# SyncE's wait for the output stores, moved from inside the block of engine programs to behind it

## What is computed

```python
x = x + L0(x, cond)   # base weight plus 8 low-rank experts, mixed by cond
x = x + L1(x, cond)   # x @ (sum over g of cond[b,g] * weight[g] * mask) + bias
x = x + L2(x, cond)   # top-2 of 8 gated-GELU experts per batch, hidden size 512, plus a shared one
x = x + L3(x, cond)   # the top-1 expert: down(silu(up(x)) * gate(x)), hidden size 256
```

## Time and profile before

| what | value |
|---|---|
| median of 3 runs | 86.92 us (86.73 to 87.36) |
| the profiled execution, its time | 87.03 us |
| its span, first to last instruction of the program | 85.2 us |
| time outside the span in that execution | 1.8 us |
| granted TensorE clock | 1.0 of full speed |
| PE busy | 82.0 us, 96% of the span |
| output stores | 8 of 64 KB each |

### The profile page before, as it was taken

The page is one execution under the profiler, slowest core; times in us unless marked ns, Lnnn a source line. Parts: engine busy times, 40 slices in busy tenths (PEclk is TensorE's granted clock), DMA queues, the critical chain, the costliest instruction groups (busy, mean ns, idle before and its releaser), DMA issues.

```text
span 85.2 us, 1938 instructions
## 1 busy us (share of the span) xinstructions
PE 82.0 (96%) x620; PEld 77.6 (91%) x620; DVE 48.5 (57%) x115; ACT 31.7 (37%) x59; POOL 15.8 (19%) x20
## 2 busy tenths in 40 slices
PE   6999999999999999999999999999999999999980
PEld 6879998888889989999999999999999999999960
DVE  1487798845336996446438428438446555463170
ACT  6502795875558401123121221221212302407450
POOL 3020298389666700000000000000000000000000
DMA  1995000699990001884879899988899898607002
GB/s 15 387 388 221 0 0 0 211 415 400 421 382 28 0 0 14 309 250 190 314 245 328 253 308 323 302 277 294 265 331 314 289 315 330 251 35 205 11 0 65
DMA packets 5336, 18.51 MB, mean 217 GB/s; under 512 B 592, under 2 KB 1744, under 8 KB 5328
## 3 DMA queue, kind: packets, MB, share of 16 engines
q1 hardware_dynamic: 5040, 17.62, 59.8%
q10 hardware_dynamic: 288, 0.79, 2.4%
HBM read 17.88 MB, written 0.52 MB: 216 GB/s over the span
## 4 chain that ended last, share of the span: by engine, by line
PE 96%; DVE 0%; issue 0%; DVEq 0%
PE bank L687 34%; PE bank L697 17%; PE bank L710 8%; PE bank L724 4%; PE bank L651 4%; PE bank L659 4%; PE bank L667 4%; PE bank L589 4%; PE bank L583 3%; PE bank L674 2%; PE bank L675 2%; PE bank L677 2%; PE bank L607 2%; PE bank L619 2%; PE bank L598 2%; DVE out_sb L504 0%
## 5 line engine op out<-in xcount | busy, mean ns | idle before, releaser
L687 PE MATMUL bank<-x_t,pair_w 128*128 128x128 f32 (+1 forms) x256 | 31.2, 276 | 0.0
L687 PEld LDWEIGHTS bank<-x_t,pair_w 128*128 128x128 f32 x256 | 29.9, 192 | 0.3
L298 ACT ACTIVATE gelu<-bank 128x512 f32<-128x512 f32 x24 | 14.2, 596 | 32.2 <-PE bank L687 28.2
L475 DVE SCALAR_TENSOR_TENSOR hid<-gelu,wsel,bank 128x512 f32<-128x512 f32 x16 | 12.0, 748 | 18.9 <-PE bank L687 18.8
L697 PE MATMUL bank<-hid,pair_w 128*128 128x128 f32 x128 | 16.9, 275 | 0.0
L697 PEld LDWEIGHTS bank<-hid,pair_w 128*128 128x128 f32 x128 | 15.6, 192 | 0.1
L262 POOL TENSOR_TENSOR hid_l<-hid,hid_h 128x512 fp32r<-128x512 f32 x8 | 10.2, 1286 | 4.3 <-ACT hid_h L326 4.3
L473 DVE TENSOR_TENSOR hid<-gelu,bank 128x512 f32<-128x512 f32 x8 | 5.5, 688 | 6.3 <-ACT gelu L298 3.8
L710 PE MATMUL bank<-x_t,w 128*128 128x128 f32 x64 | 8.5, 276 | 0.0
L710 PEld LDWEIGHTS bank<-x_t,w 128*128 128x128 f32 x64 | 7.8, 192 | 0.0
L302 ACT ACTIVATE tanh<-half 128x256 f32<-128x256 f32 x6 | 2.5, 416 | 10.1 <-DVE half L511 10.1
(11 more groups left out here) (70 smaller groups left out, 77.4 us busy)
## 6 DMA issues: line engine op xcount, KB each, us to landing
pair_w<-in_skill SPq DMA_DIRECT2D x16, 768.0 KB, 5.5
w<-in_layer SPq DMA_DIRECT2D x8, 384.0 KB, 5.5
rest_sb<-in_rest SPq DMA_DIRECT2D x1, 661.0 KB, 3.9
x_t<-in_x SPq DMA_DIRECT2D x1, 512.0 KB, 4.8
shared_sb<-in_shared ACTq DMA_DIRECT2D x1, 512.0 KB, 4.5
out_x<-out_sb SPq DMA_DIRECT2D x8, 64.0 KB, 4.4
shared_sb<-in_shared ACTq DMA_DIRECT2D x1, 256.0 KB, 4.8
head_sb<-in_head SPq DMA_DIRECT2D x1, 164.0 KB, 2.4
```

The lines of the kernel that those rows point to most:

```text
L298: act.activation(gelu[:, n, :], ps[:, :], ACT.Gelu_apprx_tanh).then_inc(gelu_ready, 1)
L475: dve.scalar_tensor_tensor(hid[:, n, :], gelu[:, n, :], wsel[:, bass.DynSlice(weight, 1)], u_ps[n][:, :], ALU.mult, ALU.mult).then_inc(hid ...
L687: mm = pe.matmul(ps[:, S * t:S * (t + 1)], pair_w[:, slot, n, 128 * t:128 * (t + 1)], x2_t[:, columns(b)], start=True, stop=True)
```

## The change

The wait becomes a function of its own, the block becomes a `with` statement that is closed before the wait, and the wait is issued on SP behind it. Its two counts and semaphores are the same.

```diff
-        block = ctx.enter_context(nc.Block())
+        def stores_landed(sp):
+
+            for q in range(2):
+                sp.wait_ge(stored[q], 16 * (B // 2))
+
+        with nc.Block() as block:
 
...
             store(B - 2, 0)
             store(B - 1, 1)
-            for q in range(2):
-                sp.wait_ge(stored[q], 16 * (B // 2))
 
...
             down3(B - 2, 0)
             down3(B - 1, 1)
 
+        stores_landed(nc.sync)
+
```

More of the change, by code:

```diff
@@ L231, in _ @@
+        def stores_landed(sp):
             for q in range(2):
                 sp.wait_ge(stored[q], 16 * (B // 2))
[L234 to L333, removed]
-            batch(1)
-            with act.Fori(1, B // 2 - 1) as j:
-                for q in range(2):
-                    batch(2 * j + q)
-            batch(B - 2)
-            batch(B - 1, last=False)
-            act.preload_act_table(ACT.Silu)
-            silu_step(B - 2, 0)
-            silu_step(B - 1, 1)
-            add_bias3(B - 2, 0)
-            add_bias3(B - 1, 1)
@@ L580, in _ @@
-        @block.tensor
-        def _(pe):
-            for _ in range(WARM):
-                pe.matmul(bank[6][:, 0:128], zeros, zeros, start=True, stop=True)
-            def mix0(first, last, mixed, count):
-                pe.wait_ge(mixed, count)
-                h, at = first // HALF, first % HALF
-                mm = pe.matmul(bank[3 + h][:, C * at:C * (at + last - first)], a_sb,
-                               b_mix[:, first:last, :].rearrange("p b o -> p (b o)"), start=True, stop=True)
-                if last % HALF == 0:
-                    mm.then_inc(p0_done, 1)
-            def mix1_part(begin, end):
-                for a in range(begin, end):
-                    h, n = a // (OL // 2), a % (OL // 2)
-                    mm = pe.matmul(bank[5 + h][:, 128 * n:128 * (n + 1)], rest_sb[:, REST + C * a:REST + C * (a + 1)], mix1[:, :], start=True, stop=True)
-                    if n == OL // 2 - 1:
-                        mm.then_inc(p1_done, 1)
-            def product0(h):
-                pe.wait_ge(p0_ready, h + 1)
-                pe.wait_ge(x_loaded, 16)
-                for n in range(HALF):
-                    b = HALF * h + n
-                    mm = pe.matmul(x1_ps[b // 2][:, S * (b % 2):S * (b % 2 + 1)], p0[:, b, :], x_t[:, columns(b)],
-                                   start=True, stop=True)
-                    if b % 2 == 1:
-                        mm.then_inc(x1_done, 1)
-            def product1(h):
-                pe.wait_ge(p1_ready, 2)
-                for n in range(HALF):
-                    b = HALF * h + n
-                    if n % 2 == 0:
-                        pe.wait_ge(x1_ready, b // 2 + 1)
-                    ps = x2_ps[n // 2][:, S * (n % 2):S * (n % 2 + 1)] if h == 0 else bank[4][:, S * n:S * (n + 1)]
-                    mm = pe.matmul(ps, p1[:, b, :], x1_t[:, columns(b)], start=True, stop=True)
-                    if n % 2 == 1:
-                        mm.then_inc(x2_done, 1)
-            pe.wait_ge(head_in, 16)
-            mix0(0, 1, b_mixed, 1)
-            mix0(1, 2, b_mixed, 2)
-            mix0(2, HALF, b_mixed, HALF)
-            mix0(HALF, B, b_mixed2, HALF)
-            pe.wait_ge(rest_landed, 16)
-            pe.wait_ge(mix1_ready, 1)
-            mix1_part(0, OL)
-            product0(0)
-            product0(1)
-            product1(0)
-            product1(1)
-            def shared_ps(k, m):
-                return ((shg_ps[k % 3], g_done), (shu_ps(k), u_done))[m]
-            def shared_high(k, m):
-                h, t = k // T, k % T
-                ps, _ = shared_ps(k, m)
-                if k >= 3:
-                    pe.wait_ge(hid_ready, k - 2)
-                if k in (1, 5):
-                    pe.wait_ge(x2_ready, 1 if k == 1 else 4)
-                if t == 0:
-                    pe.wait_ge(x2_high, 2 * (h + 1))
-                if k == 0:
-                    pe.wait_ge(sh_high, m + 1)
-                pe.matmul(ps[:, :], shared_h[:, m, 128 * t:128 * (t + 1)], x2_h[:, N * h:N * (h + 1)], start=True, stop=False)
-            def shared_middle(k, m):
-                h, t = k // T, k % T
-                ps, _ = shared_ps(k, m)
-                if k == 0:
-                    pe.wait_ge(sh_low, m + 1)
-                pe.matmul(ps[:, :], shared_l[:, m, 128 * t:128 * (t + 1)], x2_h[:, N * h:N * (h + 1)], start=False, stop=False)
-            def shared_low(k, m):
-                h, t = k // T, k % T
-                ps, done = shared_ps(k, m)
-                if t == 0:
-                    pe.wait_ge(x2_low, h + 1)
-                pe.matmul(ps[:, :], shared_h[:, m, 128 * t:128 * (t + 1)], x2_l[:, N * h:N * (h + 1)], start=False, stop=True).then_inc(done, 1)
-            def shared_down(k):
-                h, t, n = k // T, k % T, k % 3
-                if k == 0:
-                    pe.wait_ge(sh_low, 3)
-                pe.wait_ge(hid_high, k + 1)
-                pe.matmul(sh_acc[h][:, :], shared_h[:, 2, C * t:C * (t + 1)], hid_h[:, n, :], start=(t == 0), stop=False)
-                pe.matmul(sh_acc[h][:, :], shared_l[:, 2, C * t:C * (t + 1)], hid_h[:, n, :], start=False, stop=False)
-                pe.wait_ge(hid_low, k + 1)
-                pe.matmul(sh_acc[h][:, :], shared_h[:, 2, C * t:C * (t + 1)], hid_l[:, n, :], start=False, stop=(t == T - 1)
-                          ).then_inc(down_done, 1)
-            def gate_up(b, k, q):
-                slot, step = TOP_K * q + k, NSH + TOP_K * b + k
-                pe.wait_ge(pair_in[slot], 16 * fills(b, q))
-                pe.wait_ge(hid_ready, step - 1)
-                for n, (ps, done) in enumerate(((g_ps[k], g_done), (u_ps[k], u_done))):
-                    for t in range(T):
-                        mm = pe.matmul(ps[:, S * t:S * (t + 1)], pair_w[:, slot, n, 128 * t:128 * (t + 1)], x2_t[:, columns(b)],
-                                       start=True, stop=True)
-                    mm.then_inc(done, 1)
-            def down(b, k, q):
-                slot, step = TOP_K * q + k, NSH + TOP_K * b + k
-                pe.wait_ge(hid_ready, step + 1)
-                if k == 0 and at_least(b, 1):
-                    pe.wait_ge(x3_ready, b)
-                for t in range(T):
-                    mm = pe.matmul(acc_ps[:, 0:S], pair_w[:, slot, 2, C * t:C * (t + 1)], hid[:, k, S * t:S * (t + 1)],
-                                   start=(k == 0 and t == 0), stop=(k == TOP_K - 1 and t == T - 1))
-                mm.then_inc(down_done, 1)
-            def product3(b, q, n, c):
-                pe.wait_ge(w3_in[q], 16 * fills(b, q))
-                pe.wait_ge(x3_ready, b + 1)
-                if not at_least(b, 1):
-                    pe.wait_ge(x2s_ready, 2)
-                elif not is_last(b):
-                    pe.wait_ge((half3_ready, gate3_ready)[n], HC * b)
-                ps, done = ((up3_ps(b, c), up3_done), (gate3_ps(b, c), gate3_done))[n]
-                pe.matmul(ps[:, S * c:S * (c + 1)], w3[:, q, n, 128 * c:128 * (c + 1)],
-                          x3_t[:, q, :], start=True, stop=True).then_inc(done, 1)
-            def both_chunks3(b, q, n):
-                for c in range(HC):
-                    product3(b, q, n, c)
-            def down3(b, q):
-                if at_least(b, 1) and not is_last(b):
-                    pe.wait_ge(out_ready, b)
-                out_ps = out_bank(b)
-                for c in range(HC):
-                    pe.wait_ge(hid3_ready, HC * b + (c + 1 if is_last(b) else HC))
-                    mm = pe.matmul(out_ps[:, 0:S], w3[:, q, 2, C * c:C * (c + 1)], hid3[:, q, c, :],
-                                   start=(c == 0), stop=(c == HC - 1))
-                mm.then_inc(out_done, 1)
-            def batch(b, q, last=True, before_last=True):
-                gate_up(b, 0, q)
-                if last:
-                    down(b - 1, 1, 1 - q)
-                if before_last:
-                    down3(b - 2, q)
-                gate_up(b, 1, q)
-                if last:
-                    both_chunks3(b - 1, 1 - q, 0)
-                    both_chunks3(b - 1, 1 - q, 1)
-                down(b, 0, q)
-            shared_high(0, 0)
-            shared_high(0, 1)
-            shared_high(1, 0)
-            shared_high(1, 1)
-            shared_middle(0, 0)
-            shared_middle(0, 1)
-            shared_middle(1, 0)
-            shared_middle(1, 1)
-            shared_low(0, 0)
-            shared_low(0, 1)
-            shared_low(1, 0)
-            shared_low(1, 1)
-            for k in range(2, NSH):
-                for m in range(2):
-                    shared_high(k, m)
-                    shared_middle(k, m)
-                for m in range(2):
-                    shared_low(k, m)
-                if k >= 3:
-                    shared_down(k - 3)
-            gate_up(0, 0, 0)
-            gate_up(0, 1, 0)
-            shared_down(NSH - 3)
-            shared_down(NSH - 2)
-            shared_down(NSH - 1)
```

(20 more changed lines are left out.)

692 lines of the change are left out of this document (504 added, 188 removed).

## The result

| | before | after |
|---|---|---|
| median, 6 runs each on the same chips | 86.63 us (86.21 to 87.36) | 85.56 us (85.2 to 87.16) |
| ratio, 95% interval | | 0.9869 (0.9825 to 0.9913) |
| profiled execution: time, span | 87.03, 85.2 us | 85.20, 83.9 us |
| time outside the span | 1.83 us | 1.30 us |

A forecast was written before the change was run, and what follows sets the result against it. PE was taken to bound the kernel until 83.15 us, then issue, landing and barrier in series in a 2.05 us tail. Hiding the barrier takes 0.4 us from the 86.92 us median: 86.52, predicted 86.5 us, range 86.0 to 87.1.

The forecast's parts named there:

- The barrier under the landing: Program's tail: closing barrier, 0.4 us, lies wholly under the last stores' landing once SP's wait stands behind it.
- The form of the wait: SP's wait behind the block: one event now holds both counts, priced at 50 ns.
- Engines released early: Program's end: ACT, DVE, PE, POOL through 1.25 us sooner; gain taken as zero, at most 1.25 us.
- Case B: Outside the span: end hangs partly on the four engines released early; 86.1 us halfway, at most 85.7; chance 0.13.
- A: Tail: barrier hidden under the landing, 0.4 us less, 86.5 us; likeliest case, chance 0.62.
- Case C: Closing barrier: SP held until an instruction fetch brings its next instructions; gain only 0.1 us, 86.8 us; chance 0.20.
- Case D: Store landing: released engines' instruction fetches delay it; slower, up to 88.0 us with three fetches; chance 0.05.

The follow-up runs named there:

- E4: Kernel after, with the wait behind the block on POOL in place of SP; ratio to before 0.9949, 1.88 us outside the span.
- E3: Kernel after, but all five engines wait for the stores behind the block; ratio to before 0.9966, 1.90 us outside the span.
- E10: Kernel after with three empty blocks ahead of SP's wait, four barriers in all; ratio to before 0.998, 1.79 us outside the span.
- E5: Kernel after, with the wait behind the block on PE in place of SP; ratio to before 0.9931, 1.60 us outside the span.
- E9: Kernel after with two empty blocks ahead of SP's wait, three barriers in all; ratio to before 0.9955, 1.47 us outside the span.
- E2: Kernel after, unchanged, run again beside the kernel before; 85.67 against 86.48 us, ratio 0.99, 1.35 us outside the span.

## Why the prediction was wrong, point by point

*The barrier under the landing* was right in its place and its size. 0.4 us were forecast; the tail in the span fell from 2.05 to 1.65 us. SP reached its DRAIN 0.06 us behind its last issue, so the branch cost little, and the barrier took 0.35 us.

*The form of the wait* was priced at 0.05 us and took 28 ns.

*Engines released early* is the step that failed: "I take zero, since SP is the last to finish whatever is done to it". Being last in the program is not being last in the execution. Behind its last instruction POOL has 0.55 us more to go than SP (1.88 in E4 against 1.31 to 1.35), and in the kernel before both were released together, so the end was POOL's. The change makes SP later than POOL by 0.9 us, which covers the 0.55: the end passes from POOL to SP. The term was worth 0.5 us, neither zero nor the bound of 1.25. The bound was sound; the measured 0.5 is 1.82 - 1.33, and E3 gives it back entirely.

*Case B* was therefore what happened in half, with 0.13 against 0.62 for A. I had argued against it that SP has an end of its own. It has, but the argument needs SP's way to be at least as long as the others', and no row said so. The rows said nothing of the ways of the five, so the weight should have been spread from 0 to 1.25 us, and the forecast put between A and B: at 86.1 for half of B. The rule that I quoted from the Trainium skill (Runtime: NRT & Kernel Launch, The ~15µs preamble/postamble breakdown), a barrier of all engines first behind the kernel, does not carry the conclusion that I drew from it. No trace here shows what lies behind the span, so whether that barrier is there stays open. Even if it is, making all wait for the last does not make every engine's lateness cost the same, and here it does not: 1.3 to 1.9 us. Whether the five ways run side by side or are a chain with unequal steps that POOL enters first is open: both give the same maximum in E3 to E10.

*Case C* fell. The instruction fetch, seen at 84.3 before, comes in the kernel after between 83.5 and 83.9 us; the view of the DMA queues in that stretch (packets, MB, share of 16 engines):

```profile
q14 instruction: 1, 0.01, 4.8%
```

That is 0.5 us or more behind the release at 83.0, so it brought nothing that the barrier needed. *Case D* did not come about either: the last store lands 1.58 us after its issue begins, against 1.57 before, and each tail has a single instruction packet. But the landing is not as fixed as the prediction had it. It took 1.6 us in both profiles of before, in the first of after and in E5 to E9, but 1.7 us in E2 and 1.8 in E3, E4 and E10. In E3 and E10 no engine is through the program well before the landing, so an early release is not needed for it; whether one adds to it in E2 and E4 is open, and so is the cause.

*The number.* The forecast started from 86.92, the median of three runs; six runs of the same kernel gave 86.63. Of the 0.96 us between the forecast of 86.52 and the measured 85.56, 0.29 are this start, 0.5 the term taken as zero, and the rest, under 0.2, is scatter: the median moved by 1.07 us in the first comparison and by 0.81 in E2's, on both sides of the mechanism's 0.9. The spans of one kernel scatter by more than a microsecond, so six runs a side leave some tenths of doubt. The range's lower end, 86.0, would just have held the 0.9 us if they were taken from 86.92.

## What to carry to other kernels

A barrier that closes a program belongs in front of the wait for the last output stores, not behind it: 0.33 to 0.4 us of barrier then lie under the landing. To be free it must do more than end before the stores land. The engine with the longest way behind the program, here POOL, must also come to its end before the one that waits: here its release had to lie 0.55 us ahead of the end of SP's wait. With 0.95 us (one barrier) and 0.61 (two) nothing was lost, with 0.29 (three) 0.1 to 0.3 us. All of this is shown on this one kernel. Only one engine needs to wait for the stores, and which one matters, since the engines differ in what they still do behind the program: here SP was the cheapest and POOL the dearest, 0.55 us apart. When a change releases engines early at the end, the time outside the span is part of the forecast, and it should be read for both kernels, run by run, before the span's scatter is taken for an effect.

## What was unexpected of the hardware

The time outside the span stays within 1.28 to 1.39 us for the kernel after and within 1.77 to 1.93 for the kernel before, while the spans scatter by over 1 us, so it shows differences of 0.1 to 0.3 us that a median of times can't. (E9, where two engines end almost together, is the exception: 1.37 to 1.68.) It is 1.31 to 1.35 us where SP's instruction is the program's last, 1.44 with DVE's, 1.49 with ACT's, 1.60 with PE's and 1.88 with POOL's, each with whatever is timed ahead of the first instruction. Half a store of 32 KB took 2.0 us to land on SP's queue and 2.7 on ACT's, beside 1.6 us for the whole 64 KB on SP's alone. Eight equal matmuls at 3.6 us into the program took 3.1 us in one execution and 2.4 in another.
